# Half the tokens at a time: the last batch of a four-layer chain in 128-column products

## What is computed

```python
x = x + x @ W.T + 0.5 * (x @ lora_A[label]) @ lora_B.T             # layer 0
x = x + quantise(x, thresholds, deltas, zero_points)               # layer 1, elementwise, 8 groups
x = x + x @ weight[adapter].T                                      # layer 2, 1024 x 1024 per batch
x = x + (x @ B[adapter].T) @ A[adapter].T                          # layer 3, rank 16
```

## Time and profile before

| | |
|---|---|
| time before, median of 3 runs | 455.46 us (455.26 to 455.71) |
| the profiled execution's own time | 455.72 us |
| its span in the trace | 453.9 us |
| TensorE busy, matmuls / weight loads | 445.7 us (98%) / 408.0 us (90%) |
| VectorE busy | 422.6 us (93%) |
| ScalarE busy | 363.6 us (80%) |
| matmul records, and as many weight loads | 3110 |

### The profile page before, as it was taken

How to read it: one execution, slowest core, us unless ns; L and a number is a source line. 1 busy time by engine, 2 the same in 40 slices (tenths; PEclk the granted TensorE clock), 3 DMA queues, 4 the chain that set the end, 5 groups by cost and what they waited for, 6 DMA issues and landing times.

```text
span 453.9 us, 7903 instructions
## 1 busy us (share of the span) xinstructions
PE 445.7 (98%) x3110; PEld 408.0 (90%) x3110; DVE 422.6 (93%) x402; ACT 363.6 (80%) x345; POOL 51.3 (11%) x61
## 2 busy tenths in 40 slices
PE   8999999999999999999999999999999999999985
PEld 7899999889998999889998999999898989998874
DVE  4699999999999998999899998999969999999993
ACT  5699999998699768977799775997578949698840
POOL 2300010002201010000101000111100201113000
PEclk9999999999999999999999999999999999999998
DMA  7973463496368835786459835496363645679222
GB/s 253 324 293 104 84 170 88 127 236 205 82 198 219 251 88 152 196 223 219 82 184 229 242 99 152 141 221 174 72 205 108 158 120 131 182 214 329 41 92 92
DMA packets 36649, 76.94 MB, mean 169 GB/s; under 512 B 4100, under 2 KB 14724, under 8 KB 35844
## 3 DMA queue, kind: packets, MB, share of 16 engines
q1 hardware_dynamic: 30708, 61.50, 40.9%
q0 software_dynamic: 5904, 14.94, 18.6%
HBM read 53.10 MB, written 8.39 MB: 135 GB/s over the span
## 4 chain that ended last, share of the span: by engine, by line
PE 75%; DVE 16%; issue 6%; ACT 1%; DVEq 0%; POOL 0%; POOLq 0%; ACTq 0%
PE l_ps L1026 35%; PE l_ps L1133 23%; PE l_ps L1145 6%; DVE quant L889 6%; DVE cand L863 4%; DVE cand L871 2%; PE l_ps L1034 2%; PE l_ps L1182 2%; PE bx_ps L1082 2%; PE bx_ps L1201 2%; PE l_ps L1068 1%; DVE x L841 1%; DVE x L940 1%; PE l_ps L1245 1%; DVE quant L883 1%
## 5 line engine op out<-in xcount | busy, mean ns | idle before, releaser
L1133 PE MATMUL l_ps<-x,w_sb 128*128 128x256 f32 x672 | 150.2, 380 | 0.0
L889 DVE COPY_PREDICATED quant<-mask,cand 128x2048 f32<-128x2048 int8 (+2 forms) x77 | 146.2, 1898 | 0.3
L1133 PEld LDWEIGHTS l_ps<-x,w_sb 128*128 128x128 f32 x672 | 125.9, 190 | 18.3 <-issue 2.1
L660 ACT ACTIVATE cand<-x,inv_delta 128x2048 f32<-128x2048 f32 (+2 forms) x88 | 134.3, 1527 | 5.3 <-DVE quant L883 3.7
L670 ACT ACTIVATE mask<-magnitude,thr_bias 128x2048 fp8e5<-128x2048 f32 (+2 forms) x77 | 117.4, 1524 | 5.6 <-DVE quant L889 5.4
L863 DVE TENSOR_SCALAR cand<-cand,delta 128x2048 f32<-128x2048 f32 (+2 forms) x88 | 87.5, 994 | 7.4 <-ACT cand L660 7.2
L871 DVE TENSOR_SCALAR cand<-cand,lower,upper 128x2048 f32<-128x2048 f32 (+2 forms) x88 | 92.7, 1053 | 0.4
L1026 PE MATMUL l_ps<-x_hi,w_hi 128*128 128x256 f32 x496 | 82.8, 289 | 0.0
L1026 PE MATMUL l_ps<-x_hi,w_lo 128*128 128x256 f32 x496 | 79.7, 283 | 0.0
L1026 PE MATMUL l_ps<-x_lo,w_hi 128*128 128x256 f32 x496 | 79.6, 283 | 0.0
L1026 PEld LDWEIGHTS l_ps<-x_hi,w_hi 128*128 128x128 f32 x496 | 68.7, 191 | 5.0 <-issue 3.7
(11 more groups left out here) (110 smaller groups left out, 420.8 us busy)
## 6 DMA issues: line engine op xcount, KB each, us to landing
w_sb<-w SPq DMA_DIRECT2D x60, 384.0 KB, 3.8
out<-x SPq DMA_DIRECT2D x32, 256.0 KB, 2.3
x_raw<-x SPq DMA_DIRECT2D x14, 512.0 KB, 6.1
w_edge<-w SPq DMA_DIRECT2D x28, 256.0 KB, 3.8
w_lo<-w_edge POOLq DMA_DIRECT2D x28, 256.0 KB, 4.9
x_lo<-x_raw POOLq DMA_DIRECT2D x6, 1024.0 KB, 8.5
x<-a SPq DMA_DIRECT2D x7, 512.0 KB, 3.5
cand<-w SPq DMA_DIRECT2D x4, 512.0 KB, 8.2
```

Source lines behind the costliest of these rows:

```text
L660: act.activation(cand[:, c % CANDS, 0:n], x2_unit(u), ACT.Identity, bias=ROUND, scale=inv_delta[:, k:k + 1]).then_inc(rounded, 1)
L889: dve.copy_predicated(y, mask[:, m % MASKS, 0:n].bitcast(I8), t).then_inc(merged, 1)
L1133: last = nc.tensor.matmul(l2_bank(b, q)[:, i * S:(i + 1) * S], w2_block(b, o, k), x2[:, b % SLOTS, k * S:(k + 1) * S], start=(i == 0 and k ...
```

## The change

In the last batch the results of layer 2 lie by halves of the tokens: bank (t, g) of l0_ps holds, for the tokens of half t (HS = 128 columns), the four output tiles of g. In the first and the second part of layer 2 each product is issued for half 0 and then for half 1 with the same weights (`last_product`), each with 128 columns into a bank of its own. The third part goes bank by bank: (0,0), (0,1), (1,0), then the low-rank products of half 0, (1,1), and the rest of the low rank, the identity products (now one of 512 columns per half, onto bank (t, 1)) and layer 3, half by half. Low-rank results of half 0 lie in bx_ps, of half 1 in l3_ps. The split of the low-rank result, the drains, the final adds (VectorE bank (t, 0), ScalarE a copy of bank (t, 1)) and the stores go in the same halves, with semaphores of their own. The host puts the last batch's output back in order. `last_low_rank3` and `split_last_bx` are `low_rank3` and `split_bx` with 128 columns. The core of the diff:

```diff
+        def last_bank(t, g):
+            return l0_ps[:, t, g * CW:(g + 1) * CW]
+        def last_x3(t, g):
+            return x3[:, t * HW + g * CW:t * HW + (g + 1) * CW]
+        def last_tile(of, t, o):
+            return of(t, o // HALF)[:, o % HALF * HS:(o % HALF + 1) * HS]
+        def last_bx(t):
+            return (bx_ps, l3_ps)[t][:, 0:HS]
...
@@ SyncE
-            for q in LAST_ORDER:
-                store(B - 1, q)
+            for t in range(2):
+                for g in range(2):
+                    store_last(t, g)
...
@@ ScalarE
-            split_bx(B - 1)
-            for q in ADDED_UP:
-                act.wait_ge(l3_done, 4 * (B - 1) + LAST_ORDER.index(q) + 1)
-                act.activation(x3[:, q * CW:(q + 1) * CW], l3_bank(B - 1, q), ACT.Copy).then_inc(last_out_done, 1)
+            act.wait_ge(l3_done, 4 * (B - 1))
+            for t in range(2):
+                act.wait_ge(last_bx_done, t + 1)
+                act.activation(bx_split[:, t * HS:(t + 1) * HS], last_bx(t), ACT.Copy).then_inc(last_bx_hi_done, 1)
+            for t in range(2):
+                act.wait_ge(last_l3_done, 2 * t + 2)
+                act.activation(last_x3(t, 1), last_bank(t, 1), ACT.Copy).then_inc(last_copy_done, 1)
...
@@ VectorE
-            for q in range(4):
-                drain_l2(b, q)
-            split_bx(b)
-            for q in LAST_ORDER:
-                if q not in ADDED_UP:
-                    finish(b, q)
+            def drain_last(t, g):
+                dve.wait_ge(out_stored[2 * t + g], 16 * b)
+                dve.wait_ge(last_l2_done, 2 * t + g + 1)
+                of_tokens = x2[:, b % SLOTS, g * HW:(g + 1) * HW].rearrange("p (o s) -> p o s", o=HALF)
+                dve.tensor_tensor(last_x3(t, g).rearrange("p (o s) -> p o s", o=HALF),
+                                  last_bank(t, g).rearrange("p (o s) -> p o s", o=HALF),
+                                  of_tokens[:, :, t * HS:(t + 1) * HS], ALU.add).then_inc(last_x3_done, 1)
...
+            def finish_last(t):
+                dve.wait_ge(last_l3_done, 2 * t + 1)
+                dve.tensor_tensor(last_x3(t, 0), last_bank(t, 0), last_x3(t, 0), ALU.add).then_inc(last_out_done, 1)
+            for g in range(2):
+                drain_last(0, g)
+            drain_last(1, 0)
+            split_last_bx(0)
+            drain_last(1, 1)
+            split_last_bx(1)
+            finish_last(0)
+            finish_last(1)
...
@@ TensorE
+            def last_product(o, w, v, start=False):
+                for t in range(2):
+                    nc.tensor.matmul(last_tile(last_bank, t, o), w, v[:, t * HS:(t + 1) * HS], start=start, stop=False)
...
@@ last_first_part
-                        nc.tensor.matmul(l2_bank(b, o // 2)[:, o % 2 * S:(o % 2 + 1) * S], w2_block(b, o, k),
-                                         x2[:, b % SLOTS, k * S:(k + 1) * S], start=(o % 2 == 0 and k == EDGE),
-                                         stop=False)
+                        last_product(o, w2_block(b, o, k), x2[:, b % SLOTS, k * S:(k + 1) * S],
+                                     start=(o % HALF == 0 and k == EDGE))
...
-                            nc.tensor.matmul(l2_bank(b, o // 2)[:, o % 2 * S:(o % 2 + 1) * S],
-                                             w[:, k * P:(k + 1) * P], v[:, k * S:(k + 1) * S],
-                                             start=False, stop=False)
+                            last_product(o, w[:, k * P:(k + 1) * P], v[:, k * S:(k + 1) * S])
...
+            def last_second_part(tiles):
+                b = B - 1
+                pe.wait_ge(x2_done, LAST + 2)
+                for o in tiles:
+                    for k in range(PARTS[1], PARTS[2]):
+                        last_product(o, w2_block(b, o, k), x2[:, b % SLOTS, k * S:(k + 1) * S])
+            def last_third_part(t, g):
+                b = B - 1
+                for o in range(g * HALF, (g + 1) * HALF):
+                    for k in range(PARTS[2], T):
+                        last = nc.tensor.matmul(last_tile(last_bank, t, o), w2_block(b, o, k),
+                                                x2[:, b % SLOTS, k * S + t * HS:k * S + (t + 1) * HS], start=False,
+                                                stop=(o % HALF == HALF - 1 and k == T - 1))
+                last.then_inc(last_l2_done, 1)
...
+            def last_add_up(t):
+                nc.tensor.matmul(last_bank(t, 1), ident[:, :], last_x3(t, 1), start=True, stop=False)
+            def last_layer3(t, g):
+                for o in range(g * HALF, (g + 1) * HALF):
+                    last = nc.tensor.matmul(last_tile(last_bank, t, o), a3_split[:, o * P:(o + 1) * P],
+                                            bx_split[:, t * HS:(t + 1) * HS], start=(g == 0),
+                                            stop=(g == 0 or o == T - 1))
+                last.then_inc(last_l3_done, 1)
...
@@ the end of TensorE's order
-            last_layer2(1, (0,))
+            last_second_part(range(0, 2))
             sum_bx(B - 2)
-            last_layer2(1, (1, 2, 3))
+            last_second_part(range(2, T))
             layer3_pair(B - 2, 0)
             layer3_pair(B - 2, 2)
-            last_layer2(2)
-            for q in range(4):
-                low_rank3(B - 1, q)
-            for q in ADDED_UP:
-                add_up(q)
-            for q in LAST_ORDER:
-                layer3(B - 1, q)
+            pe.wait_ge(x2_done, LAST + 3)
+            last_third_part(0, 0)
+            last_third_part(0, 1)
+            last_third_part(1, 0)
+            last_low_rank3(0, 0)
+            last_low_rank3(0, 1)
+            last_third_part(1, 1)
+            last_low_rank3(1, 0)
+            last_add_up(0)
+            last_low_rank3(1, 1)
+            pe.wait_ge(a3_split_done, B)
+            pe.wait_ge(last_bx_split_done, 1)
+            for g in range(2):
+                last_layer3(0, g)
+            last_add_up(1)
+            pe.wait_ge(last_bx_split_done, 2)
+            for g in range(2):
+                last_layer3(1, g)
```

More of the change, by code:

```diff
@@ L21 @@
 HALF = T // 2
+HS = S // 2
 QUAD = 32
@@ L46 @@
 WARM = 10
-LAST_ORDER = (0, 3, 1, 2)
-ADDED_UP = (3,)
 UNITS = ((0, 0, HW), (0, HW, HW)) + tuple((b, 0, BW) for b in range(1, B - 1))\
@@ L184, in build @@
         last_out_done = sem("last_out_done")
+        last_copy_done = sem("last_copy_done")
+        last_l2_done = sem("last_l2_done")
+        last_x3_done = sem("last_x3_done")
+        last_bx_done = sem("last_bx_done")
+        last_bx_hi_done = sem("last_bx_hi_done")
+        last_bx_split_done = sem("last_bx_split_done")
+        last_l3_done = sem("last_l3_done")
         def units_of(b):
@@ L366, in store, with store_last @@
             def store(b, q):
[L367 to L372, removed]
+                sp.wait_ge(out_done, b * 4 + q + 1)
                 sp.dma_start(out[b, q], x3[:, q * CW:(q + 1) * CW]).then_inc(out_stored[q], 16)
+            def store_last(t, g):
+                sp.wait_ge((last_out_done, last_copy_done)[g], t + 1)
+                sp.dma_start(out[B - 1, 2 * t + g], last_x3(t, g)).then_inc(out_stored[2 * t + g], 16)
             def load_first_x(i, loaded):
@@ L597, in split_bx @@
             def split_bx(b):
[L598 to L601, removed]
+                act.wait_ge(bx_sum_done, b + 1)
                 if b > 0:
                     act.wait_ge(l3_done, 4 * b)
-                act.activation(bx_split[:, :], bx_whole(b), ACT.Copy).then_inc(bx_hi_done, 1)
+                act.activation(bx_split[:, :], bx_ps[:, S:2 * S], ACT.Copy).then_inc(bx_hi_done, 1)
             def split_edges(b, q):
@@ L832, in split_bx @@
                 dve.wait_ge(bx_hi_done, b + 1)
-                dve.scalar_tensor_tensor(bx_split[:, :], bx_split[:, :].bitcast(F32), not_bx_hi, bx_whole(b),
+                dve.scalar_tensor_tensor(bx_split[:, :], bx_split[:, :].bitcast(F32), not_bx_hi, bx_ps[:, S:2 * S],
                                          ALU.mult, ALU.add).then_inc(bx_split_done, 1)
@@ L844, in finish @@
                 cols = slice(q * CW, (q + 1) * CW)
-                dve.wait_ge(l3_done, b * 4 + (q if b < B - 1 else LAST_ORDER.index(q)) + 1)
+                dve.wait_ge(l3_done, b * 4 + q + 1)
                 dve.tensor_tensor(x3[:, cols], l3_bank(b, q), x3[:, cols], ALU.add).then_inc(out_done, 1)
@@ L992, in _, with split_last_bx @@
             split_a3(b)
-            for q in range(4):
-                drain_l2(b, q)
-            split_bx(b)
-            for q in LAST_ORDER:
-                if q not in ADDED_UP:
-                    finish(b, q)
+            def drain_last(t, g):
[5 more added lines that the diff above has]
+                                  of_tokens[:, :, t * HS:(t + 1) * HS], ALU.add).then_inc(last_x3_done, 1)
+            def split_last_bx(t):
+                cols = slice(t * HS, (t + 1) * HS)
+                dve.wait_ge(last_bx_hi_done, t + 1)
```

(35 more changed lines are left out.)

6 lines of the change are left out of this document (removed).

## The result

The changed kernel takes 462.0 us (median, 460.69 to 462.74) against 455.58 (455.26 to 456.09) in the same series: 1.0133 times as long, 95% interval 1.0118 to 1.0148. The medians lie 6.4 us apart, and the ratio makes it 6.1; the forecast was 7.5. The profiled execution took 461.83 us with a span of 460.1.

The account below looks back on a forecast made before the run. Bound by the ScalarE/VectorE loop until 438.02, then by TensorE's length, drains and last store. Third part +5.5 and tail +2.05 make 7.55 on a 453.9 span, 461.5; plus 1.8 less 0.3, 463.0 us; range 457.0 to 465.5.

Parts of the forecast that it names:

- The spacing: TensorE: a 128-column record behind a 128-column weight load starts 0.107 to 0.12 us after the previous; 0.12 taken, both types.
- Step 1: First part of layer 2, last batch: doubled records lengthen it from 13.0 to 19.2 us, +6.2, a 0.2 DMA wait going.
- Step 2: ScalarE's in-order copy of batch 6's low-rank sum comes 4.8 us late, delaying VectorE's loop; third part starts 5.5 later.
- T0: Start of layer 2's third part on TensorE, 438.02 before the change; forecast to move to 443.55.
- Step 3: TensorE ahead of the third part: free at 443.3, its idle stretch gone, but VectorE still ends last.
- Step 4: Behind the third part's start: third part, low rank, weight-width changes, identity products and layer 3, less waits, sum to +2.6 us.
- Step 5: Last batch's stores: two go 1.5 us ahead of the other two, so the last lands sooner, -0.55 us.
- Rival B: First part's fp32r products: the second load is cheap where weights repeat, only the tail costs; 457.6 us, chance 0.14.
- rival C: TensorE, not slower: loads hide wholly and records go at their columns' pace; 455.9 us, chance 0.09.
- D: Worse: ScalarE's late copy and the weight-width switches cost more than counted; about 466 us, chance 0.07.

Follow-up runs that it names:

- b_f32r_q: The kernel before the change, with only the first part's fp32r products issued in four of 64 columns (192 records): 488.1 us, ratio 1.0696.
- a_noadd: The changed kernel without the two identity products of 512 columns; VectorE adds all four banks, ScalarE's two copies go: 460.87 us, ratio 1.0106.
- a_early_sum: The changed kernel with batch 6's low-rank products ahead of the first part's fp32r products and sum_bx ahead of the last tile's: 461.28 us, ratio 1.0113.
- b_f32r: The kernel before the change, with only the first part's fp32r products in halves of 128 columns: 460.57 us, ratio 1.0100.
- b_f32: The kernel before the change, with only the fp32 products of the first and second part in halves of 128 columns: 455.76 us, ratio 0.9993.

## Why the prediction was right

The mechanism was the one forecast and the time lay 1.0 us under it. By its steps:

- *The spacing.* 0.12 was taken, with 0.107 as its low bound; it is 0.112, for both types. The reason for 0.12, the steady fp32r stream, was the right row and 7% too high. What b_f32r_q adds is that 64 columns have the same spacing, so it is not the columns'; that it is the load's is the reading that fits all rows, with a load's size-dependent 0.107 beside it. The Trainium skill's 81 ns for load-and-matmul pairs with 128 columns ("TensorE: Matmul & The Clock Gate", "Back-to-back issue gap") doesn't hold for these fp32 and fp32r records: 0.112 was measured. That section names no type, so "its rows are not these types" in the prediction was not read from it. The Trainium skill's section "LDWEIGHTS (loading the stationary operand)" on the same page puts a load at its weight columns divided by 1.2 GHz, 107 ns here. That is within 5 ns of the spacing, while a load's own record is 192 ns long.
- *Step 1, the first part.* 19.2 us forecast, 19.0 measured, by two errors: the records came to 17.9, and the DMA wait that was to vanish was 0.8. That the sum met the forecast is in part luck: the forecast gave no reason for the wait beyond when o = 3 comes, and it varies between runs with the same first part (0.18 in a_noadd). What the wait takes, an earlier start had given: a_noadd started 0.56 later than the changed kernel, and its third part starts at 442.80 against 442.90.
- *Step 2, who waits.* ScalarE's copy was forecast at 434.5 and came at 434.04, `split_bx` at 437.05 and 436.43, the scale at 438.7 and 438.06. The chain from there was 4.8 as said. T0 came at 442.90 instead of 443.55, so it moved by 4.9 instead of 5.5: 0.25 of the difference is the first part's earlier start (413.87 against 414.12), the rest the smaller spacing, less the longer DMA wait.
- *Step 3, TensorE right behind.* Forecast free 0.2 before VectorE, measured 0.5. a_early_sum bears it out.
- *Step 4, the tail.* +2.6 forecast, +1.8 measured. Mis-sized were the third part (+0.8, measured +0.43, by the smaller spacing) and the low rank with the changes of weight width (+0.8, measured +0.32). Four changes more cost about 0.1 each, the low end of the 0.1 to 0.2 forecast: the 16 records between two of them take 1.98, where 16 times 0.112 is 1.79. Identity products: +0.85 and +0.90. Layer 3 with what follows it: +0.15 and +0.15.
- *Step 5, the stores.* -0.55 forecast, -0.5 measured.

Rival B (457.6) is excluded by b_f32r, rival C (455.9) by the fp32r streams of 128-column records, 0.112 apart where their columns alone take 0.053; for fp32 the columns' pace, 0.108, is nearly met. D did not come. What is left open: why a steady fp32r stream of 256 columns needs 0.12 when the same load with fewer columns needs 0.112.

## What to carry to other kernels

Before splitting a matmul's moving columns, set its columns' time beside its weight load's. Here records behind a 128-column load stand 0.112 us apart: an fp32 record of 128 columns nearly fills that (0.108), and an fp32r one does not (0.053). So the same edit was free for one (b_f32) and cost 4.5 us for the other (b_f32r). And look at what stands in the in-order queues behind the lengthened stretch: a small copy on ScalarE carried TensorE's delay into VectorE's loop. Freeing it paid only 0.7 us here, since TensorE itself was late.

## What the runs showed of the hardware

A TensorE that issues without a pause can still lose its clock. In b_f32r_q, records of 64 columns at 0.112 us ran at 2.4 GHz from 423.1 to 426.8. Then they stood 0.213 apart until 461, and the granted clock was 0.50, which is 1.2 GHz, with TensorE busy all the time. With 128 columns at the same spacing it stayed at 1.00 over the whole stream, in the changed kernel (422 to 432.8) and in b_f32r, shown here in a window with the columns of the windows above:

```profile
427.00:432.50 5.50, 5.50 (x54) 5.43 (x57) 4.59 (x10) 1.82 (x3) 0.00 (x0) 1.00 0.00 0
```

So the 64-column products cost twice here: in the loads, and in the clock. The edit separates the two kernels only by the columns of a record and by their number; how narrow a record must be for this, no run shows.
